# Projection of images 2 to 15 as two packed fp32r products, with a new order of all engines

## The reference

```python
q, k, v = proj(Wq), proj(Wk), proj(Wv)            # per head: 64 channels + bias -> 64
ew = exp(w_bias * local_mask); ek = exp(k)
y = sigmoid(q) * (ew @ (ek * v)) / (ew @ ek)
h = layernorm(y @ out_w + out_b + flatten(x)) * ln_g + ln_b
h = concat([cls_tok, h])                          # 257 rows per image
u = layernorm(h); r, i = sigmoid(u @ W_r + b_r), sigmoid(u @ W_i + b_i)
a_t = sigmoid(log_a) * r; b_t = (1 - a_t) * i * (u @ W_in + b_in)
h = h + scan(h_s = a_t * h_(s-1) + b_t) @ W_out + b_out
v = layernorm(h)                                  # 8 experts 256 -> 1024 -> 256, two per token
out = h + shared(v) + sum over the two best experts of share * expert(v)
```

## Time and profile before

| what | value |
| --- | --- |
| median of three runs | 1015.47 us |
| the profiled execution | 1014.52 us |
| its span | 1012.9 us |
| mean granted TensorE clock | 0.967 of full speed |
| busy: PE, DVE, ACT, POOL | 94%, 67%, 45%, 37% |
| DMA | 82.6 MB, mean 82 GB/s |
| the mixer ends, experts start | about 559 us |

### The profile page before, as it was taken

One profiled execution on the slowest core, in us unless ns is written; L12 is line 12 of the kernel. 1 busy time (PEld: TensorE's weight loads), 2 busy tenths in 40 slices (PEclk: granted clock), 3 DMA queues, 4 the chain that ended last, 5 costly groups with the idle time before them and its releaser, 6 DMA issues.

```text
span 1012.9 us, 21761 instructions
## 1 busy us (share of the span) xinstructions
PE 950.0 (94%) x6873; PEld 889.5 (88%) x6874; DVE 676.8 (67%) x2107; ACT 460.3 (45%) x1141; POOL 379.5 (37%) x470
## 2 busy tenths in 40 slices
PE   6879999999999999999887999999999999999995
PEld 4668899888899888898886999999999999999995
DVE  3588877877778877788776465644656555554643
ACT  2214344544354453444332555555555555555552
POOL 5282432424433424334433324242433434242222
PEclk9989999999999999999988999999999999999998
DMA  9315111001111001100004727282542826473222
GB/s 266 133 34 149 43 43 43 21 21 42 42 42 42 11 31 42 42 31 22 29 35 148 204 42 214 42 213 50 122 135 43 215 45 177 83 195 59 42 42 32
DMA packets 48158, 82.61 MB, mean 82 GB/s; under 512 B 6416, under 2 KB 30883, under 8 KB 48132
## 3 DMA queue, kind: packets, MB, share of 16 engines
q0 software_dynamic: 31056, 57.46, 23.3%
q1 hardware_dynamic: 17076, 24.84, 8.3%
HBM read 55.32 MB, written 26.96 MB: 81 GB/s over the span
## 4 chain that ended last, share of the span: by engine, by line
PE 61%; issue 20%; POOL 8%; DVE 6%; ACT 2%; DMA 1%; POOLq 1%; SPq 1%; DVEq 0%; ACTq 0%
PE ps_nd L747 17%; PE ps_proj L732 14%; PE ps_ri L732 6%; PE ps_nd L909 6%; PE ps_proj L814 5%; POOL out L693 5%; PE ps_ip L732 4%; PE ps_h L897 3%; PE ps_ip L882 2%; PE ps_t L821 2%; PE ps_t L1218 1%; DVE E L1754 1%; DVE rden L1761 0%; DVE yb L1988 0%; ACT tanh_q L1290 0%
## 5 line engine op out<-in xcount | busy, mean ns | idle before, releaser
L1583 DVE TENSOR_TENSOR GL<-g_act,GH 128x256 fp32r<-128x256 f32 (+1 forms) x424 | 171.8, 418 | 176.4 <-ACT GH L1281 156.4
L1276 ACT ACTIVATE g_act<-ps_proj,fcb 128x256 f32<-128x256 f32 (+1 forms) x280 | 131.7, 470 | 301.0 <-PE ps_proj L732 272.6
L747 PE MATMUL ps_nd<-w2h,GH 128*128 128x256 f32 x832 | 241.5, 290 | 2.2 <-DVE GL L1583 2.2
L747 PE MATMUL ps_nd<-w2l,GH 128*128 128x256 f32 x832 | 234.2, 281 | 0.0
L747 PE MATMUL ps_nd<-w2h,GL 128*128 128x256 f32 x832 | 233.2, 280 | 0.0
L747 PEld LDWEIGHTS ps_nd<-w2h,GH 128*128 128x128 f32 x832 | 156.4, 188 | 6.2 <-issue 1.6
L1281 ACT CAST GH<-g_act 128x256 fp32r<-128x256 f32 x416 | 160.8, 400 | 1.1
L747 PEld LDWEIGHTS ps_nd<-w2l,GH 128*128 128x128 f32 x832 | 156.7, 188 | 0.0
L747 PEld LDWEIGHTS ps_nd<-w2h,GL 128*128 128x128 f32 x832 | 156.5, 188 | 0.0
L732 PE MATMUL ps_proj<-xh,w1h 128*128 128x256 f32 x544 | 128.1, 317 | 17.0 <-DVE E L1754 8.7
L693 POOL DMA_INDIRECT out<-yb,rows_to x72 | 114.9, 1595 | 16.7 <-issue 14.5
(11 more groups left out here) (272 smaller groups left out, 1857.4 us busy)
## 6 DMA issues: line engine op xcount, KB each, us to landing
R<-v_rows SPq DMA_DIRECT2D x37, 260.0 KB
w1h<-fc_w POOLq DMA_DIRECT2D x9, 1024.0 KB
w2h<-pj_w POOLq DMA_DIRECT2D x9, 1024.0 KB
stage<-fc_w POOLq DMA_DIRECT2D x9, 1024.0 KB
stage<-pj_w POOLq DMA_DIRECT2D x9, 1024.0 KB
v_rows<-tail_rows SPq DMA_DIRECT2D x16, 260.0 KB, 3.0
x<-x SPq DMA_DIRECT2D x16, 256.0 KB, 3.5
out<-yb SPq DMA_DIRECT2D x16, 256.0 KB
```

The source lines that it names most:

```text
L747: last = pe.matmul(banks[a], g[:, j, a * P:(a + 1) * P], w[i][:, j, :], start=(j == 0 and q == 0), stop=(j == HT - 1 and q == 2))
L1276: act.activation(g_act[:, j % G_SLOTS, 0:width], banks[j % len(banks)][:, 0:width], ACT.Gelu_apprx_tanh, bias=fcb[i][:, j:j + 1]).then_inc ...
L1583: dve.tensor_tensor(GL[:, j, 0:width], g_act[:, j % G_SLOTS, 0:width], GH[:, j, 0:width].bitcast(F32), ALU.subtract).then_inc(gl_done, 1)
```

## The change

- Images 2 to 15 are projected by two fp32r products a head. The first has 128 rows: x rounded and x's low part, both against the rounded weights (`XA`, `WA`). The second has 97: x rounded against the weights' low part, rows of ones against zeros and the rounded biases (`XB`, `WB`). POOL's queue rounds x by three loads an image (`x_high`), DVE subtracts to get the low part (`x_low`, 64 x 1024), and SP's load of x now lands in rows 64 to 127. The weights are packed once (`pack_weights`, `pack_split`, `pack_fill`). The buffers lie in the second weight set, which therefore is loaded only after the last projection.
- The cls row goes through the shared expert as two further columns of image 15 (`WIDE`, 258 columns). Its 24 output products stand ahead of the transposes of the first rows.
- The order of all engines is new; steps 14 and 15 are written out too, so the loop has steps 4 to 13. In the loop, the head of PE's step (`turn_y`, `project0`, `h_out`, `attention`, `project1`, `logits`, `hidden` 0 to 4) is as before.
- `experts` (PE, ACT) loads all eight limits first and writes the eight experts out. DVE's and POOL's loops over pairs of experts stay; `low_w` is two parts ahead.
- The cls row's copies go out by one DMA from DRAM to DRAM.

The core of the diff:

```diff
             def load_x(n, par):
-                after(sp, proj_ready, LT * (n - 1))
-                sp.dma_start(X[par][0:C, :], x[n]).then_inc(x_loaded[par], 16)
+                packed = not isinstance(n, int) or n >= 2
...
+                    sp.wait_ge(xs_done, n - 3)
+                dst = X[par][C:2 * C, :] if packed else X[par][0:C, :]
+                sp.dma_start(dst, x[n]).then_inc(x_loaded[par], 16)
...
+            def x_high(t, par):
+                n = t + 1
+                if live(n):
+                    if not isinstance(n, int) or n >= 4:
+                        pool.wait_ge(proj_ready, LT * (n - 1))
+                    pool.dma_start(XA[1 - par][0:C, :], x[n]).then_inc(xq_loaded[1 - par], 16)
+                    pool.dma_start(XA[1 - par][C:2 * C, :], x[n]).then_inc(xq_loaded[1 - par], 16)
+                    pool.dma_start(XB[1 - par][0:C, :], x[n]).then_inc(xq_loaded[1 - par], 16)
...
             def project(n, par, lt):
...
+                if packed:
+                    pe.wait_ge(xs_done, n - 1)
...
+                    if packed:
+                        cols = slice(h * 4 * D, (h + 1) * 4 * D)
+                        pe.matmul(ps_proj[:, h, :], packed_view(XA[par], lt, h), WA[:, cols],
+                                  start=True, stop=False)
+                        last = pe.matmul(ps_proj[:, h, :], packed_view(XB[par], lt, h),
+                                         WB[:, cols], start=False, stop=True)
...
+            def x_low(t, par):
+                n = t + 1
+                if live(n):
+                    dve.wait_ge(x_loaded[1 - par], 8 * (n - (1 - par)) + 16)
+                    dve.wait_ge(xq_loaded[1 - par], 24 * (n - (1 - par)))
+                    dve.tensor_tensor(XA[1 - par][C:2 * C, :], X[1 - par][C:2 * C, :],
+                                      XA[1 - par][C:2 * C, :].bitcast(F32), ALU.subtract
+                                      ).then_inc(xs_done, 1)
```

DVE's and POOL's steps, and `experts`:

```diff
             def step(t, par):
+                h_sum(t, par)
                 ekv0(t, par)
-                h_sum(t, par)
+                v_sum(t, par)
                 h_norm(t, par)
                 ekv1(t, par)
-                v_sum(t, par)
+                x_low(t, par)
                 best(t, par)
                 u_stats(t, par)
                 second(t, par)
                 u_norm(t, par)
                 ratio0(t, par)
                 u_low(t, par)
-                v_norm(t, par)
                 low(t, par, 0)
                 low(t, par, 1)
+                low(t, par, 2)
                 ratio1(t, par)
-                y_last(t, par)
...
             def step(t, par):
+                x_high(t, par)
                 rstd_h(t, par)
                 affine(t, par)
                 rstd_v(t, par)
                 rstd_u(t, par)
+                rows_out(t, par)
                 out_bias(t, par)
-                rows_out(t, par)
...
             eng.wait_ge(bounds_ready, 1)
-            with eng.Fori(0, NE // 2) as pair:
-                for i in (1, 0):
-                    g = pair * 2 + (2 - i)
-                    first = eng.value_load(bounds[0:1, bass.ds(g - 1, 1)], min_val=0,
-                                           max_val=MAX_BLK - MIN_BLKS)
...
+            limits = [0] + [eng.value_load(bounds[0:1, g:g + 1], min_val=g * MIN_BLKS,
+                                           max_val=MAX_BLK - (NE - g) * MIN_BLKS)
+                            for g in range(1, NE + 1)]
+            for g in range(1, NE + 1):
+                if start:
+                    start(g, g % 2, g // 2)
+                with eng.Fori(limits[g - 1], limits[g]) as b:
+                    block(b, g % 2, g)
```

## The result

The kernel after takes 1019.35 us (median of 6 runs, 1018.3 to 1020.9), the one before 1015.54 (1013.9 to 1016.1). The ratio is 1.0041, with a 95% interval of 1.0028 to 1.0054. I had forecast 1012.3 and called faster the likelier side, so the sign is wrong.

The account below looks back on a forecast made before the run. PE was taken to bound the kernel, with DVE 5 us slack a pass. Terms -1 + 7 + 1 - 9 + 3.3 - 3.3 - 1.2 = -3.2 took 1014.5 to 1011.3, as median 1012.3 us, range 1005 to 1020.

Parts of the forecast that it names:

- Projection: Mixer projection blocks: strided weight loads keep 8 fp32r products at 8 x 0.235 us, so zero gain; bounds 0 and -27 us.
- Rival (a): Mixer projection: strided load does not bind fp32r, -0.8 us a step in place of +0.7, 996 us; chance 13%.
- The loop's order: Steps 4 to 13: h ahead of E on DVE delays the second projection block, +0.7 us a step, +7 us.
- rival (c): Mixer steps: copies of x land after 9.5 us and hold DVE and U's transposes, 1028 us; chance 8%.
- The clock: Mixer loop: one more fall to the 1.2 GHz level in the ten steps, +1 us; bounds -7.5 and +7.5.
- rival (b): Mixer loop: the clock falls in every step behind the longer wait, 1019 us; chance 20%.
- Start: Steps 0 to 3: gains from subtractions and DMAs leaving, losses from waits for packed weights, -1 us; bounds -6 to +5.
- Steps 14 to 18: Written-out mixer steps: the new order recovers somewhat over half of about 16 us, -9 us; bounds 0 and -16.
- The way into the experts: Experts' entrance: PE's eight limit loads delay the first product, plus a likely low clock, +3.3 us; bounds -2 and +6.
- Expert boundaries: Between experts: PE's limit loads go, about 0.5 us a boundary left for DVE, -3.3 us; bounds 0 and -8.4.
- End: Kernel's end: cls row goes out in one transfer, not a load and a store, -1.2 us; bounds 0 and -2.

Follow-up runs that it names:

- E3: Kernel after, each head's tokens taken side by side from x, which changes routing, so only the mixer is read: full-clock passes 29.72 us against 30.58.
- E11: E9 with images 2 to 15 projected in f32 again and all packing copies and subtractions removed: 999.7 us, ratio 0.9853 to the kernel before.
- E1: Kernel after, with E of the first row block put back ahead of the sum h on DVE in the loop: 1011.7 us, ratio 0.9969 to before.
- E12: Kernel before, with only the sum h moved ahead of E of the first row block on DVE: 1026.0 us, ratio 1.0099.
- E4: Kernel after, second weight set's low halves subtracted by DVE in the wait for expert rows, not by POOL in steps 17 and 18: 1019.5 us.
- E5: E4 with steps 14 and 15 in the loop's order and 16 to 18 in the order of before: 1008.9 us, ratio 0.9943 to before.
- E9: Kernel after with E1's and E5's changes, and PE's and ACT's expert limits read ahead of the rows: 1000.0 us, ratio 0.9848 to before.
- E13: E9 with only the change's order of steps 14 to 18 put back on PE, ACT, DVE and POOL: 1007.4 us, ratio 0.9949 to before.
- E7: E1 plus PE's limits ahead of the rows, and x laid out by head by two ACT copies behind the first GELU: 1033.9 us, ratio 1.0190.
- E14: E9 with x laid out by head by ACT copies at its step's end, x's load ahead of the store that held it: 1014.6 us.

## Why the prediction was wrong, step by step

- **Projection: right.** Loads of 325 to 330 ns as forecast, and no gain. E3 shows the cause that I gave, E11 the value: none. Rival (a) had 0.8 less a step for a load that doesn't bind. E3's ten passes take 302.8 us, 6.9 less than before, but at full clock a pass is only 0.25 us shorter (29.72); the rest is clock, 30.6 us for a pass with a fall where before has 31.5. What binds there is DVE, as rival (a) had it, and once more ahead of U. The side-by-side loads that I called in agreement with 107 ns are so by the distance of their starts, 0.12 us; each record lasts 191 ns.
- **The loop's order: right.** +0.6 a pass where I said +0.7. E1 gives back 0.4 of it, and E12 shows the same sign in the kernel before (0.83). The 0.2 that E1 leaves is DVE's low half of x, which I had put at nothing: without the packing E11 has 29.97. DVE was busy for 27.8 us in the pass and not 25.9, mostly because its scan was held too (last section). POOL's copies of x cost nothing, as forecast: rival (c) didn't come.
- **The clock: right in size, by luck.** The ten passes took 6.8 us more, of 8 forecast for order and clock. I had forecast one more fall. It was one less: five of the ten passes had a stretch at the 1.2 GHz level, where before had six. But three of the five stretches were longer than any before (0.90 in the second pass above, 0.95 in the earlier trace rows), and that made up for it. The other five passes took 30.6 us. So rival (b), a fall in every pass, did not come, though its 1019 us is the measured time.
- **Start: wrong sign, small:** +1.9 where I took -1, inside its bounds. Not tried by itself.
- **Steps 14 to 18: this step failed.** "The new order carries image 15's transposes and output product into the step before ... I take somewhat over a half, -9 us; bounds 0 and -16." Measured +6.2, outside the bounds. That is 15.2 us too low, more than the 9.6 by which the whole sum was off (+6.4 in the profiled executions where it gave -3.2); the other steps gave some back. I counted the idle time of the old order and took a share of it as gained, with no term for what a new order loses. To compare stretches, the clock has to be taken out. In the windows a microsecond of the low level costs about half of it (1.4 us for 31.4 x 0.05 x 2 = 3.1 us in the earlier trace rows, 0.45 each). Taking that out of each stretch, with the mean clock of its window, gives (an estimate, as the 0.45 comes from the loop) 114.6 us for before, 122.6 for after, 118.6 for E4, 113.0 for E5, 112.9 for E9 and 119.7 for E13 (half a microsecond either way, as the clock has two digits). The new order alone then costs 5.6 us (E4 less E5) to 6.8 (E13 less E9), and POOL's hold on DVE 4.0 (after less E4). Before, POOL's hold cost something as well. I had not read it, as no row of mine showed POOL beside DVE, and I counted the wait that it made as idle time that an order could give back. So of the 8.0 us from before to after, by these estimates, the order alone is 5.6 to 6.8 and the rest, 1 to 2, is the hold that now falls on GL. PE's idle time says the same: 3.0 us more with the new order (E4 and E5, E13 and E9), 2.8 for the hold (after less E4).
- **The way into the experts: the parts right, the whole too high.** The eight loads took 0.7 us each where I had 0.8, and the first product stands 5.8 us behind the rows where I said 7. The 1.5 us for a low clock were not there to be lost: before had 0.77 in its window (537.44 to 559.41), after 0.78 (552.35 to 574.11). The rows came 1.4 us sooner behind the ranking, where I had expected nothing since PE waits for them anyhow. I put it down to DVE's cls copies that are gone, which was not tried.
- **Expert boundaries: mis-sized.** -3.3 forecast, -6.7 measured, within its bounds. DVE's own two loads, for which I left 0.5 us a boundary, are almost fully hidden (0.3 us at three of seven). Part of the miss is in my sum: 8.4 less seven times 0.5 is 4.9, not 3.3.
- **End: right.** -1.6 for -1.2.

What stays open: the 3.3 us wait on ACT, which of the four engines' new lists costs the 6 us (beyond the 2.2 us in image 14's pass), and the 1.9 us at the start.

## What to carry to other kernels

Before you book idle time as the gain of a new order, ask of each wait what made it, and give the new order's own waits a term. Here one of the waits came from POOL holding DVE, which no order of PE's takes away, and the new order brought 3 us of new waits of its own. Products that could run at twice the pace gained nothing here, as their weight load stayed as long; read the load's own row first, and then ask which engine is next (DVE here). The cheap finds were order ones: the producer that PE waits for goes first on its engine, register loads go ahead of a wait and not behind it, and work for a later stage goes into the wait for DMA (15 us in all, E9).

## What the runs showed of the hardware

- A DVE instruction on two SBUF operands was held for as long as POOL's subtractions ran: 0.43 became 4.53 and 4.85 us, 0.69 became 4.02 and 4.75. Two POOL subtractions in a row held one DVE instruction through both. In the loop after the change DVE's first scan took 2.57 us in place of 0.75 and ended 0.6 us behind POOL's addition of 1.29 us (L610). Beside POOL's scatter alone, before, it took 0.75.
- Reading every fourth f32 took 1.6 to 2 times as long on three engines: PE's weight load 325 to 330 ns against 195 (0.245 against 0.133 us a product), DVE's subtraction 64 x 1024 2.01 us (E7, E14) against 1.22 (after), and ACT's copy of 1024 elements 2.02 us, as long on 64 partitions as on 128, against 1.04 for a copy of 1024 that reads side by side (33 partitions, L1538 of E7).
- A register load takes 0.3 us, but eight in a row on PE's queue took from 568.4 to 573.2, 0.7 each.
